# A state-scan block on one core: the scan product ahead of the low half, the preparation spread out, fewer state copies, and another opening

## The reference

```
xn    = (x - mean) / sqrt(var + eps) * gamma + beta            # per token
delta = sigmoid(xn @ w_delta + b_delta)                        # 16 values per token
B_t   = xn @ w_in + b_in                                       # 16 values per token
gate  = sigmoid(xn @ w_gate + b_gate)                          # 512 x 512 weights
h_t   = tanh((h_{t-1} * delta_t) @ A + B_t)                    # recurrence over 2048 tokens
x     = layernorm(x + (h @ C) * gate + x)
x     = layernorm(x + real(ifft(fft(x) @ W)) + bias)           # W sparse complex 512 x 512
```

## Time and profile before

| | us |
|---|---|
| median of 3 runs (lowest, highest) | 936.36 (933.77, 939.24) |
| the profiled execution's own time | 937.29 |
| its span, first to last instruction | 935.5 |
| PE busy in it | 869.6 |
| DVE busy in it | 747.9 |
| ACT busy in it | 555.7 |
| POOL busy in it | 575.0 |

### The profile page before, as it was taken

One profiled execution on the slowest core, in us unless ns is written; L12 is line 12 of the kernel. 1 busy time (PEld: TensorE's weight loads), 2 busy tenths in 40 slices (PEclk: granted clock), 3 DMA queues, 4 the chain that ended last, 5 costly groups with the idle time before them and its releaser, 6 DMA issues.

```text
span 935.5 us, 16634 instructions
## 1 busy us (share of the span) xinstructions
PE 869.6 (93%) x5100; PEld 455.1 (49%) x5100; DVE 747.9 (80%) x1515; ACT 555.7 (59%) x1059; POOL 575.0 (61%) x906
## 2 busy tenths in 40 slices
PE   7999999998999999988888888889999999999997
PEld 4454445444455555544444444444445555555553
DVE  7888888899998888966777777779768888888883
ACT  3344444533444444534456666669768888878887
POOL 3656666687555565555555555557567777767772
PEclk8999999999999999998999999999999999999998
DMA  7579888776665668755444553456867766677753
GB/s 292 185 257 316 314 313 297 257 245 226 211 240 195 211 192 304 244 177 211 165 150 162 173 204 137 158 172 218 248 231 236 266 233 222 235 254 247 240 188 135
DMA packets 94446, 209.52 MB, mean 224 GB/s; under 512 B 4016, under 2 KB 5296, under 8 KB 90416
## 3 DMA queue, kind: packets, MB, share of 16 engines
q1 hardware_dynamic: 94096, 208.49, 64.7%
q10 hardware_dynamic: 288, 0.27, 0.1%
HBM read 139.53 MB, written 67.11 MB: 221 GB/s over the span
## 4 chain that ended last, share of the span: by engine, by line
PE 61%; DVE 16%; issue 7%; POOL 5%; ACT 5%; DMA 3%; SPq 1%; DVEq 0%; POOLq 0%; ACTq 0%
PE bank L1415 15%; PE bank L1416 15%; PE bank L1418 15%; PE bank L1405 6%; PE bank L1501 4%; DVE zh_sb L1080 3%; DVE w_ring L1309 3%; DVE gate_sb L1298 2%; ACT hi_sb L666 2%; POOL lo_sb L742 2%; PE bank L1567 2%; DVE bn L1162 1%; SPq L443 1%; DVE xs_sb L1194 1%; PE bank L1481 1%
## 5 line engine op out<-in xcount | busy, mean ns | idle before, releaser
L742 POOL TENSOR_TENSOR lo_sb<-xs_sb,hi_sb 128x512 f16<-128x512 f32 x128 | 152.0, 1187 | 159.1 <-ACT hi_sb L527 159.1
L1415 PE MATMUL bank<-wg_hi,hi_sb 128*128 128x512 f16 x512 | 196.5, 384 | 15.0 <-DVE gsum_sb L1209 9.6
L818 POOL TENSOR_TENSOR x_sb<-x_sb,gate_sb 128x512 f32<-128x512 f32 x120 | 152.7, 1273 | 76.3 <-DMA x_sb<-x 60.2
L1415 PE MATMUL bank<-w_re_sb,hi_sb 128*128 128x512 f16 x512 | 195.4, 382 | 1.8 <-DVE w_ring L1309 1.5
L1416 PE MATMUL bank<-wg_lo,hi_sb 128*128 128x512 f16 x512 | 196.3, 383 | 0.0
L1416 PE MATMUL bank<-w_re_sb,hi_sb 128*128 128x512 f16 x512 | 195.5, 382 | 0.0
L527 ACT ACTIVATE hi_sb<-xs_sb 128x512 f16<-128x512 f32 x128 | 80.5, 629 | 177.6 <-DVE xs_sb L1194 173.9
L1199 DVE SCALAR_TENSOR_TENSOR lo_sb<-bank,hi_sb 128x512 f16<-128x512 f32 x128 | 88.5, 691 | 90.4 <-ACT hi_sb L666 89.4
L1418 PE MATMUL bank<-wg_hi,lo_sb 128*128 128x512 f16 x512 | 133.6, 384 | 0.0
L1418 PE MATMUL bank<-w_re_sb,lo_sb 128*128 128x512 f16 x512 | 132.3, 381 | 0.0
L674 ACT ACTIVATE norm_sb<-x_sb,lift_bias,rstd 128x512 f32<-128x512 f32 x128 | 103.1, 805 | 22.5 <-POOL lift_bias L831 19.5
(11 more groups left out here) (184 smaller groups left out, 1392.1 us busy)
## 6 DMA issues: line engine op xcount, KB each, us to landing
x_sb<-x SPq DMA_DIRECT2D x63, 1024.0 KB, 6.2
gate_dram<-gate_sb SPq DMA_DIRECT2D x32, 1024.0 KB, 5.2
out<-out_sb SPq DMA_DIRECT2D x31, 1024.0 KB, 5.3
gate_sb<-gate_dram SPq DMA_DIRECT2D x30, 1024.0 KB, 7.0
out_sb<-x_turned SPq DMA_DIRECT2D x16, 1024.0 KB, 7.3
norm_sb<-x_turned SPq DMA_DIRECT2D x15, 1024.0 KB, 7.2
w_ring<-gate_dram SPq DMA_DIRECT2D x2, 1024.0 KB, 9.5
x_sb<-x SPq DMA_DIRECT2D x2, 512.0 KB, 5.4
```

The costliest lines, as they stand in the source:

```text
L742: pool.tensor_tensor(lo_sb[:, k % 4], xs_sb[:, k % 2], hi_sb[:, k % 4], ALU.subtract).then_inc(s_lo, 1)
L818: pool.tensor_tensor(x_sb[:, k // 4, k % 4], x_sb[:, k // 4, k % 4], gate_tile(n, k), ALU.add).then_inc(s_v, 1)
L1415: nc.tensor.matmul(dst, hi_sb[:, slot_of, t], w_hi[:, t], start=(t == 0), stop=False)
```

## The change

Four things are changed.

1. In the second pass DVE's `scan_slot(1, n)` stands behind the statistics of tile n + 4 and ahead of `low_half`, not at the end of the slot. The split of the states into halves stays at the end (`split_slot`). The check of the scan is one slot later on DVE, and its product on PE stands at the end of its slot.
2. The preparation begins at slot 42 instead of 48 and is laid out in slots that are not those of the statistics; POOL's folds are in `ROW_FOLDS` and `COLUMN_FOLDS`; the products of the pairs go through a ring of two buffers (`pq_ring`), and their high and low halves are made one slot later.
3. `replicate_states` moves two rows in one transfer: 8 transfers a group instead of 16, in two parts of four. The first part of a group is issued between the two halves of an octet, behind a wait for the split states.
4. In the opening the column sums are made from the weights as loaded, with a replicated gamma as the other factor; ACT squares the weights as loaded, scales the sums (`scaled_sums`) and copies the gate bias, to which PE has added its last part through an identity (`add_gate_bias`), so that DVE's addition is gone; the centring is split; the first tile's product takes the four high-by-high parts first (`first_gate_product`); 12 products of ones stand ahead instead of 10.

```diff
-WARM_PRODUCTS = 10
+WARM_PRODUCTS = 12
-SCAN_BRANCH = tuple(n + 2 for n in SCAN_CHECK)
+SCAN_BRANCH = tuple(n + 3 for n in SCAN_CHECK)
+ROW_FOLDS, COLUMN_FOLDS = (50, 51, 54, 55, 58, 59, 62, 63), (66, 67, 70, 71)
+WEIGHTS_HIGH = (68, 69, 72, 73)
...
-            def replicate_states(g):
-                for r in range(BATCH // 2):
-                    first = g * ROWS + r % 2 * 32
-                    for seg in range(4):
-                        src = (h_hi, h_hi, h_lo, h_lo)[seg]
-                        sp.dma_start(h_rep[32 * seg:32 * seg + 32, r, g * GROUP:(g + 1) * GROUP],
-                                     src[first:first + 32, r // 2]).then_inc(s_hrep[g][r], 16)
+            def replicate_states(g, odd):
+                first = g * ROWS + odd * 32
+                for seg in range(4):
+                    src = (h_hi, h_hi, h_lo, h_lo)[seg]
+                    sp.dma_start(h_rep[32 * seg:32 * seg + 32, odd::2, g * GROUP:(g + 1) * GROUP],
+                                 src[first:first + 32]).then_inc(s_hrep[g][odd], 16)
             for v in range(OCTETS):
                 first_pass(v, 0)
+                if v == OCTETS - 3:
+                    sp.wait_ge(s_split[0], 1)
+                    replicate_states(0, 0)
...
                 if v == OCTETS - 3:
-                    sp.wait_ge(s_split[0], 1)
-                    replicate_states(0)
+                    replicate_states(0, 1)
...
             for v in range(6):
                 second_pass(v, 0)
+                if v == 5:
+                    sp.wait_ge(s_split[1], 1)
+                    replicate_states(1, 0)
                 second_pass(v, 1)
-            sp.wait_ge(s_split[1], 1)
-            replicate_states(1)
+            replicate_states(1, 1)
...
-            PREPARATION = {
-                48: prepare_scan, 50: prepare_biases, 52: sum_weights, 55: copy_sums, 56: scale_of_w,
...
+            PREPARATION = {
+                42: prepare_scan, 43: scale_bias, 46: largest_c, 50: sum_weights, 51: largest_bias,
...
                 if exists(n + 4):
                     b_statistics(n + 4, (k + 4) % 8)
                     dve.wait_ge(s_bbn, n + 5)
+                scan_slot(1, n)
                 if exists(n + 1):
                     low_half(n + 1, k + 1, s_bhi, s_blo)
...
                 if exists(n - 1):
                     ffn_sum(n - 1, (k - 1) % 8)
-                scan_slot(1, n)
+                split_slot(1, n)
...
             def sum_gate_weights():
+                pe.wait_ge(s_grep, 1)
                 for t in range(KT):
-                    pe.wait_ge(s_gfold, t + 1)
-                    last = nc.tensor.matmul(gate_sums[:], ones_sb[:], wg_fold[:, t], start=(t == 0),
+                    pe.wait_ge(s_wg[t // (KT // 2)], 16)
+                    last = nc.tensor.matmul(gate_sums[:], gamma_rep[:, t], wg_raw[:, t], start=(t == 0),
...
+            def first_gate_product(dst):
+                def low(t):
+                    ...
+                    return nc.tensor.matmul(dst, hi_sb[:, 0, t], wg_lo[:, t], start=False, stop=(t == KT - 1))
+                pe.wait_ge(s_hi, 1)
+                for t in range(KT):
+                    pe.wait_ge(s_wg_hi, t + 1)
+                    nc.tensor.matmul(dst, hi_sb[:, 0, t], wg_hi[:, t], start=(t == 0), stop=False)
+                low(0)
+                pe.wait_ge(s_lo, 1)
+                for t in range(KT):
+                    nc.tensor.matmul(dst, lo_sb[:, 0, t], wg_hi[:, t], start=False, stop=False)
+                return [low(t) for t in range(1, KT)][-1]
```

More of the change, by code:

```diff
@@ L519, in _ @@
             act.wait_ge(s_ones, 1)
+            for t in range(KT):
+                last = nc.scalar.activation(gamma_rep[:, t], ones_sb[:], ACT.Copy, scale=gamma_sb[:, t:t + 1])
+            last.then_inc(s_grep, 1)
             for t in range(KT):
@@ L640, in slot @@
                 if isinstance(n, int) and n == -2:
-                    for t in range(1, KT):
+                    for t in range(2, KT):
                         gate_weight_high(t)
+                if isinstance(n, int) and n == -1:
+                    projections_high()
+                    gate_bias()
                 if k % 4 == 0 and exists(n - 4):
@@ L1269, in slot @@
                     row_factors(v * 2 + (k + 2) // 4, (k + 2) // 4 % 2)
-                if isinstance(n, int) and n < 1:
-                    for ahead in {-8: (0,), -7: (1,), -6: (2,), -5: (3,), -1: (4, 5), 0: (6, 7, 8)}.get(n, ()):
+                if isinstance(n, int) and n < 4:
+                    for ahead in {-8: (0,), -7: (1,), -6: (2,), -5: (3,), -1: (4, 5), 0: (6, 7), 1: (8,), 2: (9,),
+                                  3: (10, 11)}.get(n, ()):
                         a_statistics(ahead, ahead % 8, ahead // 8)
@@ L1375, in gate_bias_products, with add_gate_bias @@
                     pe.wait_ge(s_wg[part], 16)
-                    last = nc.tensor.matmul(bank[7][:], beta_rep[:, t], wg_raw[:, t], start=(t == 0),
-                                            stop=(t == KT - 1))
-                if part:
-                    last.then_inc(s_bias_mm, 1)
+                    nc.tensor.matmul(bank[7][:], beta_rep[:, t], wg_raw[:, t], start=(t == 0), stop=False)
+            def add_gate_bias():
+                pe.wait_ge(s_brow[0], 16)
+                nc.tensor.matmul(bank[7][:], ident, bias_rep[:], start=False, stop=True).then_inc(s_bias_mm, 1)
             def raise_clock():
@@ L1431, in _ @@
             raise_clock()
-            projection_bias_products()
             sum_projections()
+            projection_bias_products(0)
             pe.wait_ge(s_cst, 16)
             def products(n, k, v):
-                pe.wait_ge(s_hi, n + 1)
-                pe.wait_ge(s_lo, n + 1)
-                if before(n, 2):
-                    pe.wait_ge(s_gsum, n - 1)
-                first = isinstance(n, int) and n == 0
-                product(ps_g[k % 2][:], k % 4, wg_hi, wg_lo, gate_weights_split if first else None).then_inc(s_gate, 1)
+                if isinstance(n, int) and n == 0:
+                    first_gate_product(ps_g[0][:]).then_inc(s_gate, 1)
+                    pe.wait_ge(s_wp, 2)
+                else:
+                    pe.wait_ge(s_hi, n + 1)
+                    pe.wait_ge(s_lo, n + 1)
+                    if before(n, 2):
+                        pe.wait_ge(s_gsum, n - 1)
+                    product(ps_g[k % 2][:], k % 4, wg_hi, wg_lo).then_inc(s_gate, 1)
                 q, b = k // 4, k % 4
```

234 lines of the change are left out of this document (140 added, 94 removed).

## The result

The changed kernel takes 896.88 us (median of 4 runs, 895.66 to 897.30), the kernel before 935.07 beside it: ratio 0.959 (95% interval 0.955 to 0.963), 38.2 us less. The profiled execution took 897.30 (span 895.3, before 935.5).

A forecast was written before the change was run, and what follows sets the result against it. PE was taken as the bound, slowed in second-pass scan slots by a loop through DVE's queued scan product; gains 27.4 + 7.5 - 2 + 8.0 + 2 = 42.9 off 937.3, less 0.9, gave 893.5 us, range 880 to 911.

The forecast's parts named there:

- Scan product: Second-pass scan slots: product ahead of the low half shortens a slot from 4.68 to 3.82 us, gain 27.4 us.
- DVE becomes the bound: Rival for the second-pass scan slots: DVE's work sets 4.1 us a slot, kernel at 902.5 us; chance 0.18.
- Low half on the path: Second-pass scan slots: PE waits for the low half within the same slot, 6.1 us a slot, kernel 966; chance 0.02.
- The slower rival: Second-pass scan slots: the low half decides, 45 us more there, kernel at 966 us; chance 0.02.
- the one without effect: Rival for the scan slots: the scan waits for something else, such as transposes; kernel at 921 us; chance 0.02.
- Copies, group 0: SP's queue before the load of turned x: fewer copies send it 10 us earlier, gain 7.5 us.
- Copies, group 1: Second pass, gate load of tiles 52 to 55: added wait may stall 4.1 us; net cost 2 us.
- Preparation: First pass, tiles 48 to 119: spreading work removes half of 16.6 us of stalls, 8.3 less 0.3 us.
- The leftover of 16.6 us: First pass, tiles 48 to 119: stalls left over PE's pace and work, put down to POOL's late statistics.
- Opening: Start of the kernel: denser, rearranged work brings the first steady tile to about 30.5 us, gain 2 us.
- Signs: What the changed profile should show, such as zh_sb waits under 3 us and tanh steps of 3.75 to 3.9.

The follow-up runs named there:

- b_scan_only: Kernel before with only the second pass's scan product moved ahead of the low half (group 1's check one slot later): 905.88 us, ratio 0.968.
- a_product_third: Changed kernel with the second pass's scan product one place later, behind the low half: 901.69 us, ratio 0.960.
- b_copies_only: Kernel before with only the state copies changed, eight of two rows a group in the changed places: 927.93 us, ratio 0.992.
- a_copies_late: Changed kernel with the wait for the split and all eight copies of group 1 behind the whole octet: 891.75 us, ratio 0.953.
- a_old_tables: Changed kernel with the preparation's slots of the kernel before, ring and later halves of the pairs kept: 902.83 us, ratio 0.963.
- a_stats_first: Changed kernel with POOL's statistics ahead of the low half of the same slot, their root behind it: 891.96 us, ratio 0.953.

## Why the prediction was right, and where it was not

Predicted 893 us (range 880 to 911), measured 896.9. The total is right partly by luck, because errors cancelled: in the table above scan, copies of group 0 and opening gave 7.0 us more than forecast, preparation, copies of group 1 and the rest 9.7 less. By its steps:

*Scan product.* Forecast a slot of 3.82 us, taken above the floor of 3.76 because DVE seemed to have no slack; measured 3.70, and 31.6 us of gain instead of 27.4. PE's work alone was over-estimated by 0.06. (The long product of 0.93 us that the sum uses stands in no row shown; the earlier trace rows has 0.90. The 4.1 us of the rival isn't worked out from any.) The rival "DVE becomes the bound" (4.1 us) fell: b_scan_only, a_product_third and the changed kernel are all at 3.69 to 3.71. The Trainium skill (SBUF — State Buffer, Who interferes with whom) says that a DVE instruction with two SBUF inputs and a GpSimd instruction that reads SBUF contend. The trace agrees in the length: 0.79 us in the median where the product stands beside the addition, 0.40 behind the low half. The rest of a blocked product is shorter than a whole one: it ends 0.24 us behind the addition in the earlier trace rows and 0.25 in the slot shown above, where 0.38 is its length alone. It doesn't follow that the slot grows: the longer product falls where DVE had waited for ACT's high half anyway. DVE's waits for it in the scan slots of the second pass, before (470 to 640) and after (455 to 600):

```profile
DVE lo_sb L1199 <- ACT hi_sb L666: 42.3, 37, 2.0
```

```profile
DVE lo_sb L1249 <- ACT hi_sb L705: 4.8, 9, 1.5
```

*Low half on the path.* The slower rival didn't occur, nor did the one without effect.

*Copies, group 0.* Forecast 7.5, measured 9.0 for the stretch and 7.9 in b_copies_only for tiles 112 to 120 (23.15 us instead of 31.1). The four copies ahead of the load and h_before take 4.6 us to issue, not "some 3" (b_copies_only, rows above; 3.9 and 0.7), which the 10 us to spare covered; in the changed kernel no wait for the turned x was left.

*Copies, group 1.* The mechanism was right, a stall of 4.1 us predicted and 4.05 shown at PE. Its net cost was 4.2, not 2. PE idles 7.5 us in tiles 40 to 56 against 4.1 before, and the prediction counted the stall of the gate load alone: the x load behind it was late as well, POOL waited 10.26 us for it, and through ACT's norm_sb it cost PE another 1.10 us at 631.47. The clock is no part of the difference: it stood at 0.50 for 3.4 us in these tiles in the kernel before too (from 684.9, behind the wait at 684.25 of the earlier trace rows). The change's own later check seems to lengthen the wait by about a slot (b_copies_only), and the loss is avoidable, as a_copies_late shows.

*Preparation.* This is the step that failed: "I take half, 8.3", "less 0.3 for the slots 42 to 47". Measured 1.5 against before, 2.0 against the old tables in the same kernel. Tiles 48 to 72 did gain 3.9 us (79.6 instead of 83.5), but tiles 40 to 48, where the early work now stands, lost 2.6 and not 0.3, and tiles 72 to 96 gained nothing (91.0 instead of 90.9). The leftover of 16.6 us was put down to POOL having folds ahead of the statistics. But the waits for mean_square came from the chain tanh (from slot 70 on), high half, low half, statistics, which a table of DVE's and POOL's preparation doesn't touch: they even grew, from 11.7 to 20.0 us in tiles 40 to 112. (They are 17.7 us in a_old_tables, so most of the growth isn't from the tables; its cause is open.) a_stats_first, which changes the order and no table, removes them and gives 5.6 us.

*Opening.* Forecast 2, measured 3.3, with the steady run from 29.80 (forecast near 30.5). The 3.3 is from one pair of executions: tile 40 starts at 146.8 to 147.9 us in the three profiles with the opening of before, and at 143.9 to 147.1 in the six with the new one unaltered (three near 144, three near 147, the latter with the fall of the clock). On average that is 1.9 us; the size of this term is not known better than that.

*Signs.* PE's waits for zh_sb are 7.0 us and not under 3, but all seven lie in the first pass; in the second there is none. Tiles 48 to 72 took 79.6 us (forecast 77), the tanh steps 3.70 (forecast 3.75 to 3.9), the median product 0.79 (forecast most of them 0.9), the wait for the gate load stands where it was forecast.

## What to carry to other kernels

Here a loop through several engines cost nothing as soon as it was shorter than the slot of the engine with the most work: move its link only as far forward as that takes (behind the low half was as good as ahead of it), and don't reject a place only because the link gets longer there while the loop has slack. Before spreading work to cure a late engine, follow one of its late instructions back through the queues: if the engine was idle ahead of it, look at what it waited for and at its order before its load. In a queue that also issues loads, a wait belongs behind the loads that are due before it can be fulfilled.

## What the runs showed of the hardware

- SP's issue of a copy costs nearly the same for twice the bytes: the thirty-two copies of the kernel before took 0.59 us in the median and 0.70 on average (longest 1.65), the sixteen of double size in the changed kernel 0.61 and 0.73 (longest 1.38). In b_copies_only the eight of group 0 took 0.94 on average; what sets that wasn't tried.
- The clock that is granted after 2 us of idle time differs from execution to execution of kernels that are the same up to that point, and so the first eight tiles take 24.4 or 27.0 us.
- The granted clock of the profile can read 1.00 while matmuls of one form take 1061 ns in place of 592, so the lengths are to be read beside it. The first 4 to 7 us of the profiles looked at run at such long forms, in one execution the first 14.
